# Fused cross-attention and quantised feed-forward on one core: the transposes of an attention slot are moved behind its second scores

## The chip, the core and the metric

The kernel runs on one core of a Trainium2 chip. The metric is the device time of one execution, in microseconds (us). TensorE (PE, with its weight loads as PEld), VectorE (DVE), ScalarE (ACT), GpSimd (POOL) and the DMA queue of SyncE (SP) each work through a list of their own and meet at semaphores.

## The reference

x has the shape (2, 2048, 512), the context (2, 77, 384). All values are float32.

```python
def block(x, ctx):
    q = layernorm(x) @ Wq                 # 16 heads of 32
    k, v = ctx @ Wk, ctx @ Wv             # 77 keys
    attn = softmax(q @ k.T * 32 ** -0.5)
    x = x + tanh(g_xattn) * ((attn @ v) @ Wo)
    xq = fake_quant(layernorm(x))         # one scale over the whole tensor
    h = fake_quant(silu(xq @ wg.T) * (xq @ wu.T))
    return x + tanh(g_ffn) * (h @ wd.T)   # wg, wu, wd quantised by rows
```

## The kernel before

The 4096 rows are 32 tiles of 128. Three stages follow each other: attention, then the gate and up products, then the down product. The second stage needs the maximum over all normalised rows, so no work of it starts before the attention stage has ended.

The attention stage is a software pipeline of 36 slots. Each engine has a function `slot(n, t)`, and `tile_slots` runs it for n from 0 to 35 (slots 8 to 19 in a hardware loop). In slot n TensorE works on several tiles at once:

- `scores(n, 0)` and `scores(n, 1)`: the two halves of the heads of tile n, six products each, into the two banks of `p_s`. VectorE takes the maximum by head from them (`scores_max`, L786) and subtracts it into `prob` (`scores_sub`, L797); ScalarE takes the exponential (L632).
- `queries(n + 2, ...)`: 24 products of 256 columns into `p_q`. ScalarE rounds the result (`q_part`, L628), VectorE takes the rest (L771). In even slots they also wait for `x_part(n + 3)` on VectorE (L764), which is the last instruction of VectorE's list of the slot before.
- `prob_transpose(n - 1, 1)`: five transposes (L1129) of the second half of the probabilities, copied out of PSUM by ScalarE's `prob_copy` (L637). The first half goes another way: GpSimd splits it into planes (`prob_split`), SP transposes it by DMA (`prob_transposed`, L430), and ScalarE joins the planes (`prob_join`, L642).
- `outputs(n - 1, 0)` and `outputs(n - 1, 1)` (L1140): ten instructions each, probabilities by values. VectorE divides by the sum (`outputs_rec`, `outputs_norm`, L805 and L810).
- `out_transpose(n - 2)`: four transposes (L1156) of the attention output, taken by ScalarE (L656) and VectorE (`out_part`, L820).
- `project(n - 2)`: twelve products of 512 columns into `p_y`. VectorE adds the row (L917) and takes its statistics in slot n + 1; `row_abs` on ScalarE (L670) and `row_max` on VectorE (L878) of slot n + 2 take the maximum of the normalised row, by way of `p_y`.

Transposes and outputs have plain float32 operands; scores, queries and projection have operands split into two rounded parts, of type fp32r, and take three products for one.

The order of the work is written out by hand for each engine. Slots 4 to 29 are those in which the first half of the probabilities of tile n - 1 comes by DMA and is not the last of its kind; TensorE's list there is `behind_planes`. Slot 30 has a list of its own in that function: both transposes, both outputs, then the second scores. In slots 0 to 21 VectorE and GpSimd also quantise one 128-row block of the gate and up weights (L939, L953, L961), and in slots 22 to 29 (`down_part`, `down_scale`) the four row blocks of the down weights, whose loads SP issues (`down_rows`, L474) behind its transposes and the stores of the block before.

SP's own list does not change. It holds, for each slot, the transpose of a weight block, `planes_transposed(n + 4)`, `prob_transposed(n)` and the load of the next weight block, and `prob_transposed` waits before it starts:

```python
sp.wait_ge(g_ppl, n - PROB0 + 1)
sp.wait_ge(a_p, 2 * n)
```

`a_p` counts ScalarE's `prob_copy` and `prob_join`, two for each tile.

Of the kernel before, what the change touches and what calls it, by code (L numbers as in the profile page):

```python
# [72 lines left out]
def flamingo_block(nc, x, ctx_in, mask, g_xattn, g_ffn, Wq, Wk, Wv, Wo, clip_x, clip_down,  # L73
# [8 lines left out]
    with top:  # L82
# [30 lines left out]
        with attn:  # L113
# [17 lines left out]
            with work:  # L131
# [222 lines left out]
                def late_tile(m):  # L354
                    return isinstance(m, int) and m >= NT - 2
# [19 lines left out]
                def row(n):  # L375
                    return x1[:, span(n), :].rearrange("p a d -> p (a d)")
# [226 lines left out]
                def _(act):  # L603
# [35 lines left out]
                    def prob_join(m):  # L639
                        wait(act, d_pT, 16 * (m - PROB0) + 16)  # L640
                        wait(act, t_o, 2 * m - 1)
                        act.copy(pT_pairs, ppl_T).then_inc(a_p, 1)  # L642

                    def slot(n, t):
                        if last_by_dma(n):
                            prob_join(n - 1)
                        if isinstance(n, int) and n == 2:
                            prob_copy(n - 1, 0)
                            prob_copy(n - 1, 1)
                        if isinstance(n, int) and n in (NT - 1, NT):  # L650
                            prob_copy(n - 1, 0)
                        if runs(n - 2, NT):
                            wait(act, t_oT, n - 1)
                            if not late_tile(n - 2):
                                wait(act, t_y, n - 2)
                            act.copy(oT(n - 2)[0], p_x[:, :, :]).then_inc(a_ohi, 1)  # L656
                        if isinstance(n, int) and n == 1:
                            act.wait_ge(l_v[0], 16 * SLOT0[KB])
                        if runs(n - 1, NT) and not (isinstance(n, int) and n == 2):
                            if not by_dma(n - 1) and not (isinstance(n, int) and n in (NT - 1, NT)):  # L660
                                prob_copy(n - 1, 0)
                            prob_copy(n - 1, 1)
                        if runs(n - 4, NT - 1):
                            wait(act, g_nb2, n - 3)
                            wait(act, v_xmax, n - 3)
                            if isinstance(n, int) and n >= PLANES_FREE:
                                act.wait_ge(v_xlo, NT)
                            else:
                                wait(act, v_x1, n - 2)
                            act.activation(xabs(n - 4), row(n - 4), ACT.Abs, bias=nb2[:, span(n - 4)],  # L670
                                           scale=rs2[:, span(n - 4)]).then_inc(a_abs, 1)
# [5 lines left out]
                        if runs(n - 1, NT) and by_dma(n - 1) and not last_by_dma(n):  # L677
                            prob_join(n - 1)
# [11 lines left out]
                        if isinstance(n, int) and 1 <= n <= 4:  # L690
                            if n == 1:
                                act.wait_ge(t_v, B)
                                act.wait_ge(v_wq, KD)
                            four = slice(8 + 4 * n, 12 + 4 * n)
                            act.dma_start(x1[:, four, :], x_v[:, four, :]).then_inc(l_x[4], 16)
                        if isinstance(n, int) and n == 5:
                            act.wait_ge(g_wo, 1)
                            act.dma_start(x1[:, NT - KD:NT, :], x_v[:, NT - KD:NT, :]).then_inc(l_x[5], 16)
# [46 lines left out]
                def _(dve):  # L745
# [134 lines left out]
                    def last_slot(n, t):  # L880
# [14 lines left out]
                        dve.wait_ge(a_abs, n - 3)  # L895
                        dve.tensor_reduce(xmax[:, span(n - 4)], xabs(n - 4), X, ALU.max).then_inc(v_xmax, 1)

                    def slot(n, t):
                        if isinstance(n, int) and n == NT + 1:
                            out_part(NT - 1)  # L900
                            row_max(n - 4)
# [169 lines left out]
                def _(pe):  # L1071
# [59 lines left out]
                        last.then_inc(t_p, 1)  # L1131

                    def outputs(n, half):
                        wait(pe, a_p, 2 * n + (2 if by_dma(n) and not last_by_dma(n + 1) else 1 + half))
                        wait(pe, v_o, 2 * n - 1 + half)
                        b = n // (S // P)
                        for j in range(KB):
                            first, end = heads_of(j)
                            rows = slice(0, ROWS[j])
                            last = pe.matmul(  # L1140
                                p_o[half][:, first:end + 1, :].rearrange("p h d -> p (h d)"),
                                pT[rows, half * KB + j, :],
                                vblk[rows, span(b), half, SLOT0[j]:SLOT0[j + 1], :]
                                .rearrange("p a s d -> p (a s d)"),
                                start=(j == 0), stop=(j == KB - 1), skip_group_check=True)
# [641 lines left out]
```

## Time and profile before

| | |
|---|---|
| time, median of 3 runs | 616.19 us (615.35 to 618.91) |
| the profiled execution's own time | 615.18 us |
| its span, first to last instruction | 613.4 us |
| TensorE busy | 599.6 us, 98% of the span |
| VectorE busy | 518.3 us, 84% |
| ScalarE busy | 376.0 us, 61% |
| GpSimd busy | 234.9 us, 38% |
| slots 4 to 29 | 64.24 to 339.60 us of the span |
| second stage | its first product starts at 376.33 us |

Times in the rows are counted from the start of the span. A row of a timeline gives start, duration, engine, line and operation; the time from one start to the next tells more of a pipelined engine than the durations, which overlap. TensorE's clock was granted in full through slots 4 to 29.

### The profile page before, as it was taken

The numbers are of one execution on the slowest core, as the hardware profiler recorded it, in microseconds if no ns is written. First come the engines' busy times: TensorE is split into PE (matmuls) and PEld (weight loads), VectorE is DVE, ScalarE is ACT, GpSimd is POOL, SyncE is SP. The second block draws the span as 40 slices with busy tenths as digits, with TensorE's granted clock in tenths as the row PEclk, the third lists the DMA queues.
The fourth block names the chain that finished last, engine by engine and source line by source line (L and its number), as shares of the span: only waits on it lengthen the run. The fifth ranks groups of instructions, "written<-read, shape, count | busy, mean of one in ns | idle before, by whom it ended". The sixth has DMA issues, their size and how long they took to land. (4 is left out here: it accounts for less than half of the span.)

```text
span 613.4 us, 12115 instructions
## 1 busy us (share of the span) xinstructions
PE 599.6 (98%) x3727; PEld 446.5 (73%) x3727; DVE 518.3 (84%) x957; ACT 376.0 (61%) x484; POOL 234.9 (38%) x473
## 2 busy tenths in 40 slices
PE   8999999999999999999999997999999999899997
PEld 6799999999999999999999873444444444444544
DVE  6788899999999998999999877888888888856765
ACT  5554677777777777877775535555555554455653
POOL 6253454544544454544533112111011110067775
PEclk9999999999999999999999998999999999999999
DMA  8534785354434445534642000496642110199633
GB/s 318 172 117 119 197 193 115 84 106 89 89 89 95 95 84 109 113 70 112 139 92 61 27 1 10 114 229 219 210 173 67 35 34 1 45 368 399 251 120 120
DMA packets 118507, 77.89 MB, mean 127 GB/s; under 512 B 98211, under 2 KB 100669, under 8 KB 118461
## 3 DMA queue, kind: packets, MB, share of 16 engines
q1 hardware_dynamic: 113169, 60.51, 38.6%
q10 hardware_dynamic: 5292, 16.82, 7.4%
q8 instruction: 23, 0.38, 0.2%
q14 instruction: 23, 0.19, 0.1%
HBM read 32.48 MB, written 21.36 MB: 88 GB/s over the span
## 5 line engine op out<-in xcount | busy, mean ns | idle before, releaser
L1459 ACT ACTIVATE sb_silu<-ps_g,sb_sgu 128x512 f32<-128x512 f32 x88 | 60.5, 688 | 72.0 <-PE ps_g L1554 43.4
L1554 PE MATMUL ps_g<-sb_xqT,sb_wgu 128*128 128x512 bf16 x352 | 90.3, 379 | 0.6 <-DVE sb_xqT L1510 0.6
L1554 PE MATMUL ps_u<-sb_xqT,sb_wgu 128*128 128x512 bf16 x352 | 90.3, 379 | 0.0
L1525 DVE SCALAR_TENSOR_TENSOR sb_h<-ps_u,sb_sgu,sb_silu 128x512 f32<-128x512 f32 (+1 forms) x88 | 66.1, 751 | 19.8 <-PE ps_u L1554 19.3
L1074 PE MATMUL ps_q<-sb_xT_hi,sb_wq_hi 128*128 128x256 f32 x256 | 75.4, 294 | 0.7 <-DVE sb_xT_lo L764 0.6
L1635 POOL TENSOR_TENSOR sb_wgu<-sb_wgu,sb_x 128x512 f32<-128x512 f32 x31 | 53.6, 1730 | 52.6 <-DVE sb_wgu L1692 52.6
L632 ACT ACTIVATE sb_prob<-sb_prob 128x616 f32<-128x616 f32 x64 | 45.6, 713 | 44.3 <-DVE sb_prob L797 44.3
L1076 PE MATMUL ps_q<-sb_xT_hi,sb_wq_lo 128*128 128x256 f32 x256 | 72.4, 283 | 0.0
L1075 PE MATMUL ps_q<-sb_xT_lo,sb_wq_hi 128*128 128x256 f32 x256 | 72.3, 283 | 0.0
L1759 PE MATMUL ps_z<-sb_wdT,sb_hq 128*128 128x512 bf16 x330 | 71.9, 379 | 0.2
L1529 DVE TENSOR_REDUCE sb_hmax<-sb_h 128x1 f32<-128x512 f32 (+1 forms) x88 | 60.4, 686 | 7.6
L1554 PEld LDWEIGHTS ps_g<-sb_xqT,sb_wgu 128*128 128x128 bf16 x352 | 34.4, 98 | 42.0 <-ACT sb_xqT L1476 0.8
L1554 PEld LDWEIGHTS ps_u<-sb_xqT,sb_wgu 128*128 128x128 bf16 x352 | 34.4, 98 | 41.5
L786 DVE TENSOR_REDUCE sb_smax<-ps_s 128x8 f32<-128x616 f32 x64 | 50.9, 796 | 15.1 <-PE ps_s L1119 15.0
L1759 PEld LDWEIGHTS ps_z<-sb_wdT,sb_hq 128*128 128x128 bf16 x330 | 31.9, 98 | 39.8 <-ACT sb_hq L1655 2.3
L1442 POOL CAST sb_xqb<-sb_xq 128x512 bf16<-128x512 int8 x28 | 17.2, 614 | 112.3 <-ACT sb_xq L1451 93.7
L1655 ACT CAST sb_hq<-sb_h 128x1408 bf16<-128x1408 int8 (+1 forms) x32 | 42.0, 1312 | 28.0 <-DVE sb_h L1685 27.9
L797 DVE TENSOR_TENSOR sb_prob<-ps_s,sb_smax 128x616 f32<-128x616 f32 x64 | 51.2, 800 | 1.8
L1074 PEld LDWEIGHTS ps_q<-sb_xT_hi,sb_wq_hi 128*128 128x128 f32 x256 | 48.9, 191 | 1.4 <-DVE sb_xT_lo L764 0.8
L1074 PE MATMUL ps_y<-sb_wo_hi,sb_oT_hi 128*128 128x512 f32 x120 | 49.9, 416 | 0.0
L1075 PEld LDWEIGHTS ps_q<-sb_xT_lo,sb_wq_hi 128*128 128x128 f32 x256 | 49.0, 192 | 0.2 <-issue 0.2
L1076 PEld LDWEIGHTS ps_q<-sb_xT_hi,sb_wq_lo 128*128 128x128 f32 x256 | 48.9, 191 | 0.0
(238 smaller groups left out, 1422.7 us busy)
## 6 DMA issues: line engine op xcount, KB each, us to landing
h_spill<-sb_h SPq DMA_DIRECT2D x4, 2816.0 KB, 9.5
sb_h<-h_spill ACTq DMA_DIRECT2D x16, 704.0 KB, 7.1
out_dram<-sb_wgu SPq DMA_DIRECT2D x31, 256.0 KB, 2.2
sb_x<-in_x_dram ACTq DMA_DIRECT2D x5, 1024.0 KB, 6.1
sb_w_in<-in_L_ffn_w_gate_dram SPq DMA_DIRECT2D x11, 256.0 KB, 2.8
sb_w_in<-in_L_ffn_w_up_dram SPq DMA_DIRECT2D x11, 256.0 KB, 2.6
sb_x<-in_x_dram SPq DMA_DIRECT2D x2, 1024.0 KB, 14.0
sb_x<-in_x_dram SPq DMA_DIRECT2D x2, 512.0 KB, 4.4
```

The costliest lines, as they stand in the source:

```text
L632: act.activation(prob[:, half, :], prob[:, half, :], ACT.Exp, scale=SCALE).then_inc(a_exp, 1)
L786: dve.tensor_reduce(smax[:, half, :].rearrange("p (g h) -> p g h", g=2), half_scores(), X, ALU.max).then_inc(v_max, 1)
L797: dve.tensor_tensor(prob[:, half, :].rearrange("p (g h m) -> p g h m", g=2, h=HG), half_scores(), smax[:, half, :].rearrange("p (g h) -> p ...
L1074: pe.matmul(o, hi, rhi, start=first, stop=False)
L1075: pe.matmul(o, hi, rlo, start=False, stop=False)
L1076: return pe.matmul(o, lo, rhi, start=False, stop=last)
L1459: act.activation(silu[(j * KI + i) % 2][:, :, :].rearrange("p t n -> p (t n)"), p_g[(j * KI + i) % 2][:, :], ACT.Silu, scale=sgu[:, i:i + ...
L1525: dve.scalar_tensor_tensor(steps_h, p_u[(j * KI + i) % 2][:, :, :], sgu[:, KI + i:KI + i + 1], silu[(j * KI + i) % 2][:, :, :], ALU.mult, ...
L1529: dve.tensor_reduce(hmax[:, span(u)], steps_h, mybir.AxisListType.XY, ALU.max, apply_absolute_value=True).then_inc(v_hmax, 1)
L1554: last = pe.matmul(banks[(j * KI + i) % 2][:, :], wgu[:, what, k, i * P:(i + 1) * P], xqT[j][:, k, :], start=(k == 0), stop=(k == KD - 1))
L1635: pool.tensor_tensor(yd[k], yd[k], x1[:, span((v + RT) % NT), :].rearrange("p a d -> p (a d)"), ALU.add).then_inc(g_out, 1)
L1759: last = pe.matmul(p_z[k % 4][:, :], hq[k % 4][:, i, :], wdT[:, i, :], start=(i == 0), stop=(i == KI - 1))
```

## The change

In slots 4 to 29 TensorE's list is put in another order. Before: first scores, transposes of the output, transposes of the probabilities, queries, second scores, a quarter of the projection, both outputs, the rest of the projection. After: first scores, queries, second scores, transposes of the output, transposes of the probabilities, both outputs, the whole projection. `outputs` now waits for each half's own count of `a_p`.

ScalarE gets a list for these slots, `planes_slot`: the join of the planes comes first (before, it followed the first exponential), so it counts in `a_p` ahead of `prob_copy`; the copy of the transposed output and `prob_copy` come behind `q_part` instead of at the slot's head.

VectorE gets one too: the addition of the row comes ahead of the first maximum, the rest of the queries ahead of the second maximum, and `out_part` between the second maximum and its subtraction. The instructions and their numbers are the same on every engine. The cut diff:

```diff
 # tensor
 def behind_planes(n, t):
-        out_transpose(n - 2)
-        prob_transpose(n - 1, 1)
         if last_by_dma(n):
+            out_transpose(n - 2)
+            prob_transpose(n - 1, 1)
             outputs(n - 1, 0)
...
                 queries(n + 2, (t + 2) % 4, part)
         scores(n, t, 1)
-        project(n - 2, [0])
+        out_transpose(n - 2)
+        prob_transpose(n - 1, 1)
         outputs(n - 1, 0)
         outputs(n - 1, 1)
-        project(n - 2, range(1, KD))
+        project(n - 2)
 def outputs(n, half):
-        wait(pe, a_p, 2 * n + (2 if by_dma(n) and not last_by_dma(n + 1) else 1 + half))
+        wait(pe, a_p, 2 * n + 1 + half)
 # scalar
+def planes_slot(n, t):
+        prob_join(n - 1)
+        if runs(n - 4, NT - 1):
+            row_abs(n - 4)
+        exponential(n, 0)
+        if runs(n + 2, NT):
+            q_part(n + 2, (t + 2) % 4)
+        out_high(n - 2)
+        prob_copy(n - 1, 1)
+        if runs(n + 4, NT):
+            x_join(n + 4, t)
+        exponential(n, 1)
+        if runs(n + 5, NT):
+            normalise(n + 5, t + 5)
 # vector
+def planes_slot(n, t):
+        m = n - 3
+        wait(dve, t_y, m + 1)
+        dve.tensor_tensor(row(m), y_full(m)[:, 0:D], row(m), ALU.add).then_inc(v_x1, 1)
+        scores_max(n, 0)
+        wait(dve, v_x1, m + 1)
+        wait(dve, v_st2, m)
+        scores_sub(n, t, 0)
+        dve.bn_stats(bn2[:, 0, :], row(m)).then_inc(v_bn2, 1)
+        wait(dve, v_bn2, m + 1)
+        wait(dve, g_nb2, m)
+        if runs(n - 4, NT):
+            row_max(n - 4)
+        dve.bn_aggr(mvt[:, :], bn2[:, 0, :]).then_inc(v_st2, 1)
...
+        down_part(n, 0)
...
+        if runs(n + 2, NT):
+            q_part(n + 2, (t + 2) % 4)
+        scores_max(n, 1)
+        out_part(n - 2)
+        scores_sub(n, t, 1)
...
+        outputs_rec(n - 1, 0)
+        outputs_norm(n - 1, 0)
+        outputs_rec(n - 1, 1)
...
```

## Rows read from the trace of the kernel before

**Rows 1.** Windows, slots 4 to 21 and 22 to 29: length, then busy time by engine.

```profile
64.24:254.59 190.35, 190.35 (x1387) 180.69 (x1386) 175.76 (x360) 142.33 (x180) 91.92 (x232) 1.00 0.51 109
254.59:339.60 85.01, 85.01 (x617) 80.24 (x616) 80.01 (x163) 59.16 (x75) 36.24 (x85) 1.00 0.46 99
```

**Rows 2.** Waits, 60 to 330 us: who waited for whom, total, times, longest.

```profile
DVE sb_smax L786 <- PE ps_s L1119: 11.2, 20, 1.9
```

**Rows 3.** Timeline of TensorE, slot 13: transposes, then queries.

```profile
160.66 0.71 PE L1129 MATMUL ps_p<-sb_identf,sb_prob 128*128 128x128 f32 x5
161.13 0.36 PE L1074 MATMUL ps_q<-sb_xT_hi,sb_wq_hi 128*128 128x256 f32 x1
161.33 0.28 PE L1075 MATMUL ps_q<-sb_xT_lo,sb_wq_hi 128*128 128x256 f32 x1
161.45 0.28 PE L1076 MATMUL ps_q<-sb_xT_hi,sb_wq_lo 128*128 128x256 f32 x1
```

**Rows 4.** Timeline of TensorE, slot 3: transposes before outputs, scores before queries.

```profile
55.99 0.71 PE L1129 MATMUL ps_p<-sb_identf,sb_prob 128*128 128x128 f32 x5
56.53 1.23 PE L1140 MATMUL ps_o<-sb_vblk,sb_pT 128*128 128x66 f32 x10
...
58.36 0.30 PE L1119 MATMUL ps_s<-sb_k_hi,sb_q_lo 128*128 128x308 f32 x1
58.50 0.28 PE L1074 MATMUL ps_q<-sb_xT_hi,sb_wq_hi 128*128 128x256 f32 x1
```

**Rows 5.** Timeline of TensorE, slot 12: outputs, then the projection's rest.

```profile
156.12 1.28 PE L1140 MATMUL ps_p<-sb_vblk,sb_pT 128*128 128x66 f32 x10
157.20 0.48 PE L1074 MATMUL ps_y<-sb_wo_hi,sb_oT_hi 128*128 128x512 f32 x1
157.52 0.39 PE L1075 MATMUL ps_y<-sb_wo_lo,sb_oT_hi 128*128 128x512 f32 x1
157.75 0.40 PE L1076 MATMUL ps_y<-sb_wo_hi,sb_oT_lo 128*128 128x512 f32 x1
```

**Rows 6.** Timeline of slot 30, TensorE, its weight loads and ScalarE.

```profile
341.43 1.23 PE L1140 MATMUL ps_o<-sb_vblk,sb_pT 128*128 128x66 f32 x10
342.50 1.28 PE L1140 MATMUL ps_p<-sb_vblk,sb_pT 128*128 128x66 f32 x10
342.44 1.20 PEld L1140 LDWEIGHTS ps_p<-sb_vblk,sb_pT 128*128 128x128 f32 x10
341.63 0.69 ACT L637 COPY sb_pT<-ps_p 128x640 f32<-128x640 f32 x1
```

**Rows 7.** Waits of the SP queue, 60 to 340 us.

```profile
SPq L429 <- ACT sb_pT L642: 66.1, 26, 8.2
```

**Rows 8.** The tile sb_ppl, 100 to 300 us: DMA from issue to landing.

```profile
DMA to landing us min/median/max: 3.3/3.3/4.1
```

**Rows 9.** Timeline of VectorE, turn of slots 12 and 13.

```profile
159.42 0.66 DVE L764 TENSOR_TENSOR sb_xT_lo<-sb_xpl,sb_xT_hi 128x512 fp32r<-128x512 f32 x1
160.43 0.80 DVE L786 TENSOR_REDUCE sb_smax<-ps_s 128x8 f32<-128x616 f32 x1 [0.35 <-PE ps_s L1119]
161.14 0.68 DVE L917 TENSOR_TENSOR sb_x<-ps_y,sb_x 128x512 f32 x1
```

**Rows 10.** Timeline of VectorE, slot 22: its maxima and a subtraction; slots 23, 24.

```profile
255.64 0.80 DVE L786 TENSOR_REDUCE sb_smax<-ps_s 128x8 f32<-128x616 f32 x1 [0.68 <-PE ps_s L1119]
...
260.36 0.80 DVE L786 TENSOR_REDUCE sb_smax<-ps_s 128x8 f32<-128x616 f32 x1
261.19 0.80 DVE L797 TENSOR_TENSOR sb_prob<-ps_s,sb_smax 128x616 f32<-128x616 f32 x1
...
266.57 0.79 DVE L786 TENSOR_REDUCE sb_smax<-ps_s 128x8 f32<-128x616 f32 x1
...
276.88 0.80 DVE L786 TENSOR_REDUCE sb_smax<-ps_s 128x8 f32<-128x616 f32 x1
...
302.86 0.69 DVE L827 TENSOR_REDUCE sb_wd_am<-sb_w_in 128x1 f32<-128x512 f32 x1 [0.71 <-DMA sb_w_in<-in_L_ffn_w_down_dram]
```

More of the change, by code:

```diff
@@ L642, in prob_join, with x_load @@
                         act.copy(pT_pairs, ppl_T).then_inc(a_p, 1)
-                    def slot(n, t):
+                    def x_load(n):
+                        if isinstance(n, int) and 1 <= n <= 4:
+                            if n == 1:
+                                act.wait_ge(t_v, B)
+                                act.wait_ge(v_wq, KD)
+                            four = slice(8 + 4 * n, 12 + 4 * n)
+                            act.dma_start(x1[:, four, :], x_v[:, four, :]).then_inc(l_x[4], 16)
+                        if isinstance(n, int) and n == 5:
+                            act.wait_ge(g_wo, 1)
+                            act.dma_start(x1[:, NT - KD:NT, :], x_v[:, NT - KD:NT, :]).then_inc(l_x[5], 16)
@@ new lines, in row_abs @@
+                    def row_abs(m):
+                        wait(act, g_nb2, m + 1)
+                        wait(act, v_xmax, m + 1)
+                        if isinstance(m, int) and m + 4 >= PLANES_FREE:
+                            act.wait_ge(v_xlo, NT)
+                        else:
+                            wait(act, v_x1, m + 2)
+                        act.activation(xabs(m), row(m), ACT.Abs, bias=nb2[:, span(m)],
+                                       scale=rs2[:, span(m)]).then_inc(a_abs, 1)
@@ new lines, in out_high @@
+                    def out_high(m):
+                        wait(act, t_oT, m + 1)
+                        if not late_tile(m):
+                            wait(act, t_y, m)
+                        act.copy(oT(m)[0], p_x[:, :, :]).then_inc(a_ohi, 1)
+                    def planes_slot(n, t):
[12 more added lines that the diff above has]
+                            normalise(n + 5, t + 5)
@@ L645, in slot @@
+                    def slot(n, t):
+                        if by_dma(n - 1) and not last_by_dma(n):
+                            planes_slot(n, t)
+                            if isinstance(n, int) and n in (4, 5):
+                                x_load(n)
+                            return
                         if last_by_dma(n):
@@ L652, in slot @@
                         if runs(n - 2, NT):
[L653 to L656, printed above, removed]
+                            out_high(n - 2)
                         if isinstance(n, int) and n == 1:
@@ L663, in slot @@
                         if runs(n - 4, NT - 1):
[L664 to L671, printed above, removed]
+                            row_abs(n - 4)
                         if runs(n, NT):
@@ L676, in slot @@
                             act.copy(wo_hi[:, :, :], wo_raw).then_inc(a_wo, 1)
-                        if runs(n - 1, NT) and by_dma(n - 1) and not last_by_dma(n):
-                            prob_join(n - 1)
                         if runs(n + 2, NT):
@@ L689, in slot @@
                             normalise(n + 5, t + 5)
[L690 to L698, printed above, removed]
+                        if isinstance(n, int) and 1 <= n <= 3:
+                            x_load(n)
                     act.dma_start(mask_u, mask.rearrange("(a b) m -> a (b m)", a=1)).then_inc(l_mask, 16)
@@ L896, in last_slot @@
                         dve.tensor_reduce(xmax[:, span(n - 4)], xabs(n - 4), X, ALU.max).then_inc(v_xmax, 1)
+                    def planes_slot(n, t):
[12 more added lines that the diff above has]
+                        dve.bn_aggr(mvt[:, :], bn2[:, 0, :]).then_inc(v_st2, 1)
+                        if runs(n, NW):
+                            wait(dve, d_w, 16 * n + 16)
+                            wait(dve, g_sc, n)
+                            dve.tensor_reduce(w_am[:, :], w_in[:, :], X, ALU.max, apply_absolute_value=True)\
+                               .then_inc(v_wam, 1)
+                        down_part(n, 0)
+                        if runs(n, NW):
+                            wait(dve, v_wam, n + 1)
+                            wait(dve, v_wi8, n)
+                            dve.reciprocal(w_inv[:, :], w_am[:, :]).then_inc(v_winv, 1)
+                        if runs(n + 2, NT):
[3 more added lines that the diff above has]
+                        scores_sub(n, t, 1)
+                        if runs(n, NW):
+                            wait(dve, v_winv, n + 1)
+                            wait(dve, g_wbf, n)
+                            dve.tensor_scalar(w_i8[:, :], w_in[:, :], w_inv[:, :], QMAX, ALU.mult, ALU.mult)\
+                               .then_inc(v_wi8, 1)
+                        down_part(n, 1)
+                        down_part(n, 2)
+                        down_scale(n)
+                        if runs(n + 6, NT):
+                            wait(dve, v_st, n + 6)
+                            if isinstance(n, int) and n + 6 == 12:
+                                dve.wait_ge(l_x[4], 16 * 4)
+                            if isinstance(n, int) and n + 6 == NT - KD:
+                                dve.wait_ge(l_x[5], 16)
+                        outputs_rec(n - 1, 0)
+                        outputs_norm(n - 1, 0)
+                        outputs_rec(n - 1, 1)
+                        if runs(n + 6, NT):
+                            stats(n + 6)
+                            wait(dve, v_bn, n + 7)
+                            wait(dve, g_nb, n + 5)
+                        outputs_norm(n - 1, 1)
+                        if runs(n + 6, NT):
+                            stats_end(n + 6, t)
+                        if runs(n + 4, NT):
+                            x_part(n + 4, t)
@@ L898, in slot @@
                     def slot(n, t):
+                        if by_dma(n - 1) and not last_by_dma(n):
+                            planes_slot(n, t)
+                            return
                         if isinstance(n, int) and n == NT + 1:
```

## The prediction

> **What bounds the kernel now.** I read the windows first: in slots 4 to 21 TensorE is busy for the whole 190.35 us, VectorE for 175.76, ScalarE for 142.33; the clock is full [rows 1]. Divided by 18 that is 10.575 us a slot, of which VectorE fills 9.76 by the same row. In slots 22 to 29 TensorE is again busy throughout, but the slot is 85.01 / 8 = 10.626 us: 8 x 0.051 = 0.41 us of stretched products hide there, and VectorE is at 80.01 of 85.01. Then the waits: VectorE waits for the scores of TensorE, 11.2 us in 20 waits, and no wait of TensorE of any size stands against it [rows 2]. So TensorE's issue sets the slot, VectorE is 0.4 to 0.6 us behind it, and the change can win only if TensorE's own list gets shorter, or lose if a new order makes TensorE wait. The timelines then say what one switch costs and how late each partner may be. Nothing after slot 29 changes; the second stage waits for all rows, so a microsecond of a slot is a microsecond of the end.
>
> **TensorE's list.** The same instructions are issued; only the neighbours change. The removed neighbourhood is transposes to queries. It looks dear: the first query takes 0.36 us against 0.28, and the next one starts 0.20 us later instead of 0.12 (161.13, 161.33, 161.45) [rows 3]. But the five transposes before it take only 161.13 - 160.66 = 0.47 us from start to start, while in front of outputs the same five take 56.53 - 55.99 = 0.54 [rows 4]. Both together: 0.47 + 0.20 = 0.67 with the switch, 0.54 + 0.12 = 0.66 without. The cost is 0.01 us; most of what one row shows is given back by the row ahead. The dearer switch is outputs to projection: 1.08 + 0.32 us against 1.07 + 0.23, some 0.10 us [rows 5, 6], and the new order keeps one of it a slot. Scores to queries, which is new here, costs 0.14 us, the ordinary spacing of scores [rows 4]. The whole slot, from starts: scores 12 x 0.141 = 1.69, queries 24 x 0.12 = 2.88, nine transposes 9 x 0.108 = 0.97, outputs 1.07 + 1.08 = 2.15, projection 0.32 + 11 x 0.2325 = 2.88 (0.23 is 157.75 - 157.52). Sum 10.57 us, against 10.575 now. I take -0.015 us x 26 = -0.4 us. Bounds: -0.08 x 26 = -2.1 us if the first query's 0.08 is all real, +0.02 x 26 = +0.5 us for the rounding of the rows.
>
> **The new short path: transposes, copy, outputs.** Call the start of the first scores 0. Then queries start at 0.85, second scores at 3.73, output transposes at 4.58, probability transposes at 5.01, outputs at 5.55 and 6.62, projection at 7.70. Before, some 4.5 us lay between the probability transposes and the outputs that use them; now the second outputs follow 1.6 us behind, and `prob_copy` lies between, queued on ScalarE behind `q_part` and the copy of the output. Slot 30 of the old kernel has just this order. There the copy starts at 341.63 and ends at 342.32, the weight load that needs it is at 342.44, and the outputs start at 342.50, 1.07 us behind the first ones (341.43), which is their own length [rows 6]. So the wait is nothing, with 0.12 us from the copy's end to the load. That holds if ScalarE is free when the transposes end: `q_part` starts at about 3.95 (queries end) and ends at 4.55; the copy of the output can start at 5.21. I take 0. Bounds 0 and, if the copy came 0.1 us later in each slot, 26 x 0.1 = +2.6 us.
>
> **SP and the join.** `prob_transposed(n)` waits until `a_p` is 2n. Today the last to count is the join (66.1 us of waits in 26 slots) [rows 7], 5.7 us into the slot. With the join first, the last to count is `prob_copy`, which ends at 6.45: the transposing DMA starts 0.7 us later. It lands 3.3 us behind its issue, 4.1 at worst [rows 8], so at 9.8 to 10.6. The join wants it when ScalarE is through its list, at about 9.7, some 0.1 us late, at worst 0.9. Behind the join stand `row_abs` (`row_max` wants it at 3.3 of the next slot, it ends at 1.7) and the first exponential, which waits for VectorE until 2.7 anyway. The loop join, `row_abs`, exponential, `q_part`, two copies, DMA is about 4.6 + 3.4 = 8.0 us round, under 10.57. Queued on SP behind this DMA are the next weight load and weight transpose; their own waits end later (8.0 and 8.8), so they keep their times. Cost 0.
>
> **VectorE, slots 4 to 21.** The addition now starts at 0.20, when the projection ends, where the first maximum had to wait until 160.43, 1.05 into its slot [rows 9]. The list gets waits on itself: maximum then subtraction with nothing between costs 261.19 - 260.36 = 0.83 us instead of about 0.71 (161.14 - 160.43) [rows 9, 10]; `row_max` straight behind the statistics, and the reciprocal straight behind its maximum, I estimate at the same 0.11 each. So +0.2 to +0.3 us a slot on a list that ended 0.35 us before the slot did: it comes to about 10.35 of 10.57, idle included. TensorE's deadlines against it: even queries want `x_part` by 0.72 of the slot, and it ends near 0.05 (before: 160.08, that is 0.70, wanted at 1.70); second scores want the subtraction by 3.6, it ends at 2.7; the projection wants `out_part` by 7.56, it ends at 6.9. Cost 0; bound above: 0.1 us a slot, 18 x 0.1 = +1.8 us.
>
> **VectorE, slots 22 to 29.** Here it has no slack: from first maximum to first maximum slot 22 takes 10.93 us and slot 23 10.31, without a wait [rows 10]. The pair is 21.24 against TensorE's 21.15. The new waits add about 0.15 (two of 0.11 to 0.12 come, one goes since `out_part` parts the second pair): 11.08 and 10.46. How late VectorE begins a slot, L: 0 at slot 22, then 0.14 idle + 11.08 - 10.57 = 0.65 at 23, 0.54 at 24. Even queries are the tight deadline, since they moved 0.9 us forward: `x_part` ends at 0.27 + L, plus 0.05 to be seen, wanted by 0.72, so L above 0.40 is paid. Slot 24 pays 0.14, L is 0.91 at 25, slot 25 some 0.1 for `out_part`, slot 26 0.35. Then the loads of the down weights: in slot 26 the first reduction waits 0.71 us for DMA until 302.86, 5.8 into the slot [rows 10]; it is now due at 4.3, and the rest of the queries, the second maximum and `out_part` (0.60 + 0.60 + 0.72 + 0.73 us) stand behind it, so the projection goes at 8.45 instead of 7.56: 0.9 us. Loads of the other three blocks landing near their old time I price at 0.3 together. Sum 0.14 + 0.1 + 0.35 + 0.9 + 0.3 = 1.8, less the 0.41 that is lost now [rows 1]: +1.4 us. Bounds: -0.4 if no lag is left, +3.0 if each of three loads costs what slot 26's does.
>
> The Trainium skill ("VectorE: DVE Perf Modes", The DRAIN you can't avoid) says that chained VectorE instructions cost the same with a semaphore after each as without. By that rule the 0.15 a slot would be gone and L would stay near 0.5 at slot 24 and 0.7 at slot 26, the lag near 0.3 us instead of 0.6, and the sum 0.3 lower. The pair at 0.83 against 0.71 speaks against it.
>
> **Sum.** -0.4 + 0 + 0 + 0 + 1.4 = +1.0 us. The profiled execution took 615.18 us (span 613.4), so 616.2 for it; it lies 1.0 us under the median of 616.19, so I forecast **617.2 us** for the median, +0.16%. A measurement of this kernel tells about 0.5%, 3.1 us, from no change.
>
> **Rivals.**
> (1) The switch is real: TensorE gains the 0.08 us of the first query in 26 slots, -2.1 us, and the lag of slots 22 to 29 vanishes because `out_transpose` no longer waits for VectorE's division, -0.4: 613.7 us, faster by 0.4%. For it: the 0.36 us row. Against: the 0.47 ahead of it [rows 3, 4].
> (2) The second outputs wait for `prob_copy`. The margin is 0.12 us [rows 6]; it decides as soon as ScalarE begins the copy of the output over 0.1 us late. With 0.2 us a slot: +5.2 + 1.0 = 622.4 us, slower by 1.0%. Against: ScalarE has 0.65 us idle ahead of that copy.
> (3) VectorE becomes the bound in slots 4 to 21 too: its list is 0.2 us under the slot; if three more self-waits or a late weight load add 0.35, the slot is 10.7: 18 x 0.15 + 1.0 = 619.9 us.
> (4) The loads of slots 22 to 29 land early enough: the 0.9 + 0.3 go, 616.0 us. For it: slot 26's is the only such wait of the old trace [rows 10].
>
> **Chances.** Forecast 0.42; (4) 0.16; (1) 0.14; (2) 0.13; (3) 0.15. The range must reach (1) and (3) and the lower part of (2): 613.6 to 621.0; the likeliest case alone has 616.0 to 618.9. Faster by over 0.5% (below 613.1) needs (1) and more: 0.09. Slower by over 0.5% (above 619.3) is (2), over half of (3) and the top of the forecast's bound: 0.25. The rest, 0.66, is no change.
>
> **What would show it.** Right: in slots 5 to 21 output transposes start 10.56 to 10.58 us apart; five transposes before outputs 0.54 us, queries 0.12 throughout; second outputs 1.07 us behind the first; SP's L429 waits for L637 instead of L642; small stretches of TensorE before even queries and before the projection in slots 24 to 27, and VectorE's L827 waiting for DMA longer than 0.71 us. Wrong: a slot of 10.50 or less, or of 10.7 or more, before slot 22; a wait of L1140's weight load for ScalarE L637.

## The result and the profile after

The kernel after the change takes **618.22 us** (median of 20 runs, 616.76 to 622.82); the kernel before, on the same chip, 615.73 us (20 runs, 615.02 to 620.21). The ratio is 1.0037, with an interval of 1.0023 to 1.0051: 2.5 us slower. That is too little to tell from no change by the bound of 0.5%, and 1.0 us above the forecast of 617.2. The profiled execution took 617.91 us, span 616.0, so 2.73 us more than the profiled execution of before.

The page's first part, busy time by engine:

```profile
PE 601.0 (98%) x3727; PEld 447.6 (73%) x3727; DVE 519.5 (84%) x957; ACT 382.2 (62%) x484; POOL 234.8 (38%) x473
```

The shares hardly moved. ScalarE has 6 us more, 4 of them in slots 4 to 29; where they come from isn't shown, its join has kept its mean length of 1.66 us. The difference is found by stage. The windows of after, slots 4 to 21, slots 22 to 29, and then slot 28 by itself:

```profile
64.51:255.08 190.57, 190.57 (x1387) 180.74 (x1386) 176.91 (x360) 146.38 (x181) 91.17 (x232) 1.00 0.50 109
255.08:342.80 87.72, 86.23 (x618) 80.70 (x617) 80.11 (x163) 59.16 (x74) 36.41 (x85) 1.00 0.43 96
...
320.09:332.19 12.10, 10.80 (x78) 10.12 (x77) 9.20 (x20) 7.05 (x9) 3.42 (x8) 1.00 0.42 117
```

Against [rows 1] the first eighteen slots take 190.57 us for 190.35, 0.2 us more, and TensorE is busy for all of it. The last eight take 87.72 for 85.01: 2.7 us, the whole difference. What follows slot 29 is the same, 26.62 us from slot 30 to the last product of the stage for 26.63. Slot by slot, from the first product of the first scores to that of the next slot, in us:

| slot | 22 | 23 | 24 | 25 | 26 | 27 | 28 | 29 | sum |
|---|---|---|---|---|---|---|---|---|---|
| before | 10.59 | 10.65 | 10.59 | 10.65 | 10.59 | 10.78 | 10.58 | 10.58 | 85.01 |
| after | 10.58 | 10.91 | 10.95 | 11.03 | 10.94 | 10.60 | 12.10 | 10.61 | 87.72 |

There are two losses: slots 23 to 26 are each 0.3 to 0.45 us over a free slot of 10.58 (1.5 us together), and slot 28 is 1.5 us over.

TensorE in slot 13 of after, to be laid beside [rows 3 to 5]; start, duration, line and operation, with groups of equal rows cut:

```profile
160.46 0.30 PE L1206 MATMUL ps_s<-sb_k_hi,sb_q_lo 128*128 x1
160.60 0.28 PE L1161 MATMUL ps_q<-sb_xT_hi,sb_wq_hi 128*128 128x256 f32 x1
160.72 0.28 PE L1162 MATMUL ps_q<-sb_xT_lo,sb_wq_hi 128*128 128x256 f32 x1
...
164.31 0.60 PE L1243 MATMUL ps_x<-sb_identf,sb_o_sb 128*128 128x128 f32 x4
164.75 0.71 PE L1216 MATMUL ps_p<-sb_identf,sb_prob 128*128 128x128 f32 x5
165.29 1.23 PE L1227 MATMUL ps_o<-sb_vblk,sb_pT 128*128 x10
166.36 1.29 PE L1227 MATMUL ps_p<-sb_vblk,sb_pT 128*128 x10
167.46 0.47 PE L1161 MATMUL ps_y<-sb_wo_hi,sb_oT_hi 128*128 128x512 f32 x1
167.77 0.39 PE L1162 MATMUL ps_y<-sb_wo_lo,sb_oT_hi 128*128 128x512 f32 x1
```

The first query is now 0.28 us long and the next one starts 0.12 us later, but the five transposes take 165.29 - 164.75 = 0.54 us where they took 0.47. The second outputs start 1.07 us behind the first and the projection 1.10 behind them: no wait for `prob_copy`.

The waits of after between 60 and 345 us (who for whom: total, times, longest):

```profile
ACT sb_pT L642 <- DMA sb_ppl<-sb_ppl: 9.6, 23, 2.2
DVE sb_prob L825 <- DVE sb_smax L814: 5.2, 26, 0.2
DVE sb_wd_am L855 <- DMA sb_w_in<-in_L_ffn_w_down_dram: 3.0, 4, 2.3
DVE sb_smax L814 <- PE ps_s L1206: 2.6, 7, 1.6
PEld ps_y L1161 <- DVE sb_oT_lo L848: 1.6, 2, 1.4
PE ps_y L1161 <- DVE sb_oT_lo L848: 1.3, 1, 1.3
PEld ps_q L1161 <- DVE sb_xT_lo L792: 0.7, 2, 0.3
```

VectorE's waiting for the scores has shrunk: over 60 to 330 us it was 11.2 [rows 2] and is 0.9; the 2.6 shown here have 1.6 from slot 30. In its place stand 26 waits of 0.2 us on its own maximum, and 3.0 us on loads of the down weights: 0.20 in slot 22, 0.24 in slot 24, 0.26 in slot 26 and 2.30 in slot 28. ScalarE's join now waits for its DMA in 23 slots, 9.6 us in all, where the kernel before had one such wait of 0.9; TensorE has no wait on ScalarE among its own. It now waits for VectorE, at the projection (1.3) and at the even queries (0.7, seen on its weight loads). The bound is still TensorE, but in slots 23 to 26 and in slot 28 VectorE now holds it up.

VectorE of after at the start of slot 13, in slots 23 and 24 and in slot 28 (in brackets the idle time ahead of an instruction, and what ended it):

```profile
160.18 0.68 DVE L929 TENSOR_TENSOR sb_x<-ps_y,sb_x 128x512 f32 x1
160.80 0.80 DVE L814 TENSOR_REDUCE sb_smax<-ps_s 128x8 f32<-128x616 f32 x1
161.80 0.80 DVE L825 TENSOR_TENSOR sb_prob<-ps_s,sb_smax 128x616 f32<-128x616 f32 x1 [0.20 <-DVE sb_smax L814]
...
270.59 1.11 DVE L863 TENSOR_SCALAR sb_w_i<-sb_w_in,sb_wd_inv 128x512 int8<-128x512 f32 x1
...
281.16 0.17 DVE L939 BATCH_NORM_AGGREGATE sb_mvt<-sb_bn 128x2 f32<-128x6 f32 x1
281.57 0.69 DVE L855 TENSOR_REDUCE sb_wd_am<-sb_w_in 128x1 f32<-128x512 f32 x1 [0.24 <-DMA sb_w_in<-in_L_ffn_w_down_dram]
...
326.65 0.69 DVE L855 TENSOR_REDUCE sb_wd_am<-sb_w_in 128x1 f32<-128x512 f32 x1 [2.30 <-DMA sb_w_in<-in_L_ffn_w_down_dram]
327.26 0.68 DVE L799 TENSOR_TENSOR sb_q_lo<-ps_q,sb_q_hi 128x512 fp32r<-128x512 f32 x1
327.85 0.79 DVE L814 TENSOR_REDUCE sb_smax<-ps_s 128x8 f32<-128x616 f32 x1
328.56 0.68 DVE L848 TENSOR_TENSOR sb_oT_lo<-ps_x,sb_oT_hi 128x512 fp32r<-128x512 f32 x1
```

Four things are to be seen. From maximum to subtraction it is now 161.80 - 160.80 = 1.00 us, where the prediction took 0.83; the maximum, though, starts 0.62 us behind the addition, where the addition started 0.71 behind the maximum before. The scaling to int8 of slot 23 takes 1.11 us, where the same place of the list took 0.74 before. In slot 24 the reduction of a down block starts 281.57 - 281.16 = 0.41 us behind the instruction ahead of it, because it waits for its load. And in slot 28 the reduction of a down block waits 2.30 us for its load, with the rest of the queries, the second maximum and `out_part` queued behind; `out_part` ends at 329.24, 9.15 us into the slot, and TensorE's projection has stood still for it:

```profile
326.71 1.28 PE L1227 MATMUL ps_p<-sb_vblk,sb_pT 128*128 128x66 f32 x10
329.30 0.50 PE L1161 MATMUL ps_y<-sb_wo_hi,sb_oT_hi 128*128 128x512 f32 x1 [1.30 <-DVE sb_oT_lo L848]
```

Why that load is late is read on SP's queue and on GpSimd. SP of after ahead of slot 28 (the second column is the issue's length), then its counterpart of before, then GpSimd of after:

```profile
316.01 1.35 SPq L430 DMA_TRANSPOSE sb_ppl<-sb_ppl  x1
317.40 4.60 SPq L480 DMA_DIRECT2D wd_spill<-sb_w_bf  x2
322.05 0.43 SPq L474 DMA_DIRECT2D sb_w_in<-in_L_ffn_w_down_dram  x1
```

```profile
313.72 1.35 SPq L430 DMA_TRANSPOSE sb_ppl<-sb_ppl  x1
315.74 3.32 SPq L480 DMA_DIRECT2D wd_spill<-sb_w_bf  x2
319.11 0.43 SPq L474 DMA_DIRECT2D sb_w_in<-in_L_ffn_w_down_dram  x1
```

```profile
321.03 0.62 POOL L577 CAST sb_w_bf<-sb_vblk 128x512 bf16<-128x512 int8 x1 [4.33 <-DMA wd_spill<-sb_w_bf]
```

SP issues the transpose of the probabilities later in the slot (6.5 to 6.9 us into it, before 5.7 to 6.1), because it waits for `prob_copy` instead of the join: 94.0 us in 26 slots where it was 66.1 [rows 7]. Behind it stand the two stores of the quantised block. The second store needs GpSimd's second cast, the cast needs the first store landed (4.33 us of waiting, where it was 2.38 before), and the next load stands behind the second store. The load is issued 1.96 us into slot 28, before 0.67. So 1.3 of the 2.30 us are the later issue; the rest is that VectorE, with its new list, is at the reduction 4.3 us into the slot, before 5.0.

### The profile page after: what moved, and what is told of

It reads as the page before. It is cut to its first block and busy times, and to the rows that moved or that the text cites. A ratio compares the mean times of both kernels' runs of the same rounds, so it can differ in the third digit from the quotient of the medians.

```text
span 616.0 us, 12121 instructions
## 1 busy us (share of the span) xinstructions
PE 601.0 (98%) x3727; PEld 447.6 (73%) x3727; DVE 519.5 (84%) x957; ACT 382.2 (62%) x484; POOL 234.8 (38%) x473
## 5 line engine op out<-in xcount | busy, mean ns | idle before, releaser
L1612 DVE SCALAR_TENSOR_TENSOR sb_h<-ps_u,sb_sgu,sb_silu 128x512 f32<-128x512 f32 (+1 forms) x88 | 66.1, 751 | 19.7 <-PE ps_u L1641 18.8
L1161 PE MATMUL ps_q<-sb_xT_hi,sb_wq_hi 128*128 128x256 f32 x256 | 73.3, 286 | 1.0 <-DVE sb_xT_lo L792 0.6
L642 ACT COPY sb_pT<-sb_ppl 128x1280 uint16<-128x1280 uint16 x27 | 44.9, 1662 | 9.6 <-DMA sb_ppl<-sb_ppl 9.6
```

What stands on the lines that cost most here:

```text
L1161: pe.matmul(o, hi, rhi, start=first, stop=False)
L1612: dve.scalar_tensor_tensor(steps_h, p_u[(j * KI + i) % 2][:, :, :], sgu[:, KI + i:KI + i + 1], silu[(j * KI + i) % 2][:, :, :], ALU.mult, ...
```

## The experiments

In each table the slots are those of the profiled execution. Its load times scatter: one or two of the slots 26 to 28 may be 1 to 2 us longer or shorter in another execution, so the row of slots tells where time is lost and the ratio tells how much. Slots 4 to 21 took 190.4 to 190.6 us in all that keep the new lists, and are not repeated.

**old_tail.** The new order in slots 4 to 21 only; slots 22 to 29 have the old lists on all engines.

```diff
-if by_dma(n - 1) and not last_by_dma(n):
+if by_dma(n - 1) and not last_by_dma(n) and n < 22:      # on every engine
```

> Slots 4 to 21 as changed, slots 22 to 29 with the old lists on all three engines. Theory A (the whole loss is made in slots 22 to 29, where VectorE is full and the down weights are loaded): the 2.7 us lost there come back, slots 4 to 21 keep their 10.58 us, and the kernel is within 0.1% of the one before the change, 615.5 to 616.3. Rival B (the new order itself costs, spread over all 26 slots, or after them): slots 4 to 21 hold two thirds of it, and the kernel stays some 1.5 us over the one before.

Measured: 616.29 us against 615.72, ratio 1.0014 (0.9992 to 1.0037); windows, slots 22 to 29:

```profile
255.06:340.44 85.38, 85.02 (x618) 80.26 (x617) 79.61 (x163) 59.00 (x74) 36.25 (x85) 1.00 0.45 99
```

Slots 4 to 21 keep 190.57 us, and the eight last ones are back at 85.38; the 0.37 us over the kernel before are all in slot 27 (11.16 for 10.78), behind a wait for a load of 1.10 us in slot 26. Where VectorE has slack the new order costs no more than 0.2 us in eighteen slots and gains nothing; the loss lies in slots 22 to 29.

**sp_join.** SP's transpose waits for the join only, as it did before.

```diff
-sp.wait_ge(a_p, 2 * n)
+sp.wait_ge(a_p, 2 * n - (n > PROB0))
```

> The changed kernel, but SP's transpose of the probabilities waits for the join alone (2n - 1), not for the copy behind it. Theory A: the DMA starts about 5.0 us into a slot instead of 6.5, the stores and loads of the down weights queued behind it go 1 to 3 us earlier, the 2.3 us wait of VectorE in slot 28 goes and with it the 1.5 us of that slot; the lag of slots 23 to 26 (some 1.5 us) stays: 1.2 to 1.6 us faster than the changed kernel, about 1.0 us over the one before. Rival C (the late load of slot 28 is contention of transfers, not the queue): the wait moves or stays, no gain.

**max_first.** In slots 23 to 26 the first maximum goes ahead of the addition, so that VectorE has an instruction between maximum and subtraction.

```diff
+if 23 <= n <= 26: scores_max(n, 0)
 dve.tensor_tensor(row(m), y_full(m)[:, 0:D], row(m), ALU.add)
-scores_max(n, 0)
+if not 23 <= n <= 26: scores_max(n, 0)
```

> The changed kernel, but in slots 23 to 26 VectorE takes the first maximum ahead of the addition, so that the addition stands between the maximum and its subtraction. Theory A: each of the four slots gets 0.2 to 0.28 us of VectorE back, TensorE's stretch in them falls from 1.5 us to about 0.5, slot 28 keeps its 1.5: 0.8 to 1.1 us faster than the changed kernel. Rival D (these slots are late for the queries' wait on x_part or another engine, whatever VectorE's length): no change in slots 23 to 26.

**both.** The two edits together.

> Both edits, the wait for the join alone and the first maximum ahead in slots 23 to 26. Theory A: they add up, 2.2 to 2.6 us faster than the changed kernel, within 0.1% of the one before. If TensorE's order were worth anything by itself, this kernel would be faster than the one before; by the rows it is worth 0.0 +/- 0.5 us.

| | median (before) | ratio | slots 22 to 29 |
|---|---|---|---|
| sp_join | 616.98 | 1.0027 (1.0009 to 1.0044) | 10.58, 10.89, 10.96, 10.66, 10.93, 10.60, 10.65, 10.59 = 85.86 |
| max_first | 618.62 | 1.0053 (1.0032 to 1.0073) | 10.58, 10.59, 10.94, 11.21, 10.96, 10.60, 11.37, 10.60 = 86.85 |
| both | 616.74 | 1.0013 (0.9995 to 1.0032) | 10.58, 10.71, 10.93, 10.58, 10.94, 10.58, 10.81, 10.58 = 85.71 |

The windows of sp_join, slots 22 to 29:

```profile
255.53:341.39 85.86, 85.70 (x618) 80.59 (x617) 79.98 (x163) 59.35 (x74) 36.67 (x85) 1.00 0.42 99
```

With SP's earlier wait, slot 28 falls from 12.10 to 10.65 and the wait for its load from 2.30 to 0.84 us. One execution of each could be scatter, so all kernels are laid side by side. With SP's early wait (here, in `both` and in the next two) the load is issued 0.86 to 1.31 us into slot 28, VectorE waits 0.84 to 1.56 us for it and the slot takes 10.65 to 11.36. With the late wait (after, `max_first`, `more_switches`) it is 1.43 to 1.96, 1.56 to 2.30 and 11.37 to 12.10. The second loss is SP's wait for the larger part.

Slots 23, 24 and 26 keep their loss, but slot 25 falls from 11.03 to 10.66. That is a load too. In slot 24 the reduction now finds its block landed, and VectorE's list of that slot is shorter by 0.37 us (10.96 for 11.33, from addition to addition):

```profile
281.60 0.17 DVE L939 BATCH_NORM_AGGREGATE sb_mvt<-sb_bn 128x2 f32<-128x6 f32 x1
281.69 0.65 DVE L855 TENSOR_REDUCE sb_wd_am<-sb_w_in 128x1 f32<-128x512 f32 x1
```

`max_first` missed what was expected of it: it frees slot 23 (10.91 to 10.59) and no more, and its median isn't below that of the changed kernel. The edit itself is worth some 0.18 us in slot 23, as `both` shows against `sp_join` (10.71 for 10.89); the rest of the 0.32 lies in a wait for the load of slot 22 that this execution didn't have. In slot 24 VectorE, being earlier, waits 0.68 us for the load instead of 0.24, and slot 25 takes 11.21. Slots 24 and 26 stay at 10.93 to 10.96 in both kernels that have the edit: there the queries wait for `x_part`, at the end of VectorE's list. `both` was expected 2.2 to 2.6 us faster than the changed kernel; it is so by 1.5 us in the medians and 2.0 in the slots.

**join_xpart.** As sp_join, and `x_part(n + 4)`, which the even queries of the next slot wait for, goes ahead of `outputs_rec` from slot 22 on.

```diff
+if n >= 22: x_part(n + 4, t)
 outputs_rec(n - 1, 0)
...
-x_part(n + 4, t)
+if n < 22: x_part(n + 4, t)
```

> The kernel in which SP waits for the join alone, and in slots 22 to 29 VectorE takes the rest of the transposed row (x_part) ahead of the four reciprocals and divisions instead of at the end of its list, some 1.9 us earlier. Theory A (even slots pay because their queries, moved 0.9 us forward, wait for x_part): slots 24 and 26 fall from 10.95 to about 10.6; the lag itself stays, so slots 23 and 25 still pay for out_part or the second scores, 10.7 to 10.9. Slots 22 to 29 take 85.2 to 85.5 us instead of 85.86. Rival E (even slots pay for something else that is behind VectorE): slots 24 and 26 stay at 10.9.

Measured: 617.10 us against 615.79, ratio 1.0020 (1.0000 to 1.0041); slots 10.58, 10.91, **10.59**, 11.03, 10.87, 10.80, 11.04, 10.60 = 86.42. Slot 24 is free at once, so its 0.37 us had been the deadline of the even queries, as the prediction had it. Slots 23 and 25 keep their loss; 0.21 us of it in each lies ahead of the projection, which wants `out_part`, the rest at the second scores. The sum was expected at 85.2 to 85.5 and missed it, because VectorE waits 0.25, 0.55 and 1.23 us for loads in slots 22, 26 and 28. It isn't earlier at the reduction of slot 26 than in `sp_join` (4.77 us into the slot, 4.67 there); the block is there later, 5.4 us behind its issue.

**all_three.** SP's wait, the maximum first, and the early `x_part`.

> The wait for the join alone, the first maximum ahead in slots 23 to 26, and x_part ahead of the divisions in slots 22 to 29. Theory A: no deadline of TensorE is missed by more than 0.1 us, slots 22 to 29 take 84.7 to 85.1 us, the same as before the change (85.01); the time equals the one before within 0.1%. Rival B (the new order of TensorE costs by itself): over 85.5.

Measured: 618.04 us against 615.79, ratio 1.0034 (1.0021 to 1.0047); slots 10.58, 10.64, 10.59, 10.79, **11.96**, 10.81, 11.36, 10.60 = 87.33. The expectation was missed. The first four slots are nearly free, but the gain is given back: VectorE's reduction waits for loads, 3.4 us in three waits, the longest 1.7 us in slot 26. There SP's issue of the load takes 2.07 us; in all other blocks of this run it is 0.43 to 0.52. What held it isn't shown.

```profile
DVE sb_wd_am L855 <- DMA sb_w_in<-in_L_ffn_w_down_dram: 3.4, 3, 1.7
```

```profile
298.23 2.07 SPq L474 DMA_DIRECT2D sb_w_in<-in_L_ffn_w_down_dram  x1
```

**late_down.** The changed kernel, with the first block work of slots 22, 24, 26 and 28 behind the second subtraction, so that nothing TensorE wants soon is queued behind the wait for the load.

```diff
-down_part(n, 0)
+if wd_step(n)[1] != 0: down_part(n, 0)
 ...
 scores_sub(n, t, 1)
+if wd_step(n)[1] == 0: down_part(n, 0)
```

> The changed kernel, but in slots 22, 24, 26 and 28 VectorE's first reduction of the down weights (down_part 0) moves from ahead of the queries' rest to behind the second subtraction, beside the other two. Theory A: in these slots nothing that TensorE waits for stands behind the load any more; the waits of VectorE for it (3.0 us in four slots, 2.3 of them in slot 28) shrink under 0.3, slot 28 falls from 12.1 to about 10.6 us; slots 23 to 26 keep most of their lag. Slots 22 to 29 take 86.0 to 86.4 us instead of 87.7, and the kernel is 1.2 to 1.6 us faster than the changed one. Rival F (the load's landing is only the sign of a late store chain that holds something else up): slot 28 stays over 11.

Measured: 617.05 us against 616.09, ratio 1.0027 (1.0006 to 1.0047); slots 10.58, 10.96, 10.97, 10.89, 10.96, 10.60, **10.60**, 10.60 = 86.16. VectorE's wait for loads is gone, though SP still waits for `prob_copy`. Slots 23 to 26 lose as much as in the changed kernel; in slots 22 and 28 a wait of 0.27 and 0.28 us for ScalarE's part of the queries stands where the wait for the load was. So the second loss goes without the first, as in slots 22 to 25 of `all_three` the first went without the second.

**all_four.** All of these together.

> All four edits: SP waits for the join alone, first maximum ahead in slots 23 to 26, x_part ahead of the divisions and down_part 0 behind the second subtraction in slots 22 to 29. Theory A: slots 22 to 29 take 84.7 to 84.9 us, which is TensorE's own list, against 85.01 before the change; the kernel's time equals the one before within 0.1%, so that the order of TensorE is worth nothing and everything the change lost was waits. Rival B: over 85.5 us, or a slower kernel all the same.

Measured: 616.01 us against 616.09, ratio 1.0005 (0.9979 to 1.0031); slots 10.58, 10.74, 10.60, 10.77, 10.60, 10.58, 10.58, 10.58. Windows, slots 4 to 21 and 22 to 29:

```profile
64.69:255.27 190.58, 190.58 (x1388) 180.74 (x1386) 176.76 (x360) 144.87 (x181) 91.53 (x232) 1.00 0.50 109
255.27:340.30 85.03, 85.03 (x617) 80.40 (x616) 80.22 (x163) 59.00 (x74) 37.20 (x85) 1.00 0.43 100
```

TensorE is busy for all of both stretches, and they are as long as before the change within 0.2 us [rows 1]. The last eight slots stay 0.13 us above the 84.9 that were expected at most; slots 23 and 25 still lose 0.16 and 0.19. With the two losses away or nearly so the new order of TensorE is worth 0: it equals the kernel before and doesn't beat it.

**more_switches.** One run. The changed kernel, with the output transposes between the two halves of the queries: each slot has one more pair of changes between plain float32 and fp32r.

```diff
 for part in range(2):
     queries(n + 2, (t + 2) % 4, part)
+    if part == 0: out_transpose(n - 2)
 scores(n, t, 1)
-out_transpose(n - 2)
```

> The changed kernel, but the four transposes of the output stand between the two halves of the queries in slots 4 to 29, which puts one more switch from float32 to fp32r products into each slot. By the prediction a switch behind transposes costs 0.01 us: slots 4 to 21 at 10.58 to 10.60. Rival 1 of the prediction (0.08 us of the first product behind it are real): 10.66 or more, 1.5 us over slots 4 to 21. The query behind the transposes should last 0.36 us and have its neighbour 0.20 us behind it in either case.

Measured: 617.46 us, one run; slots 4 to 21 190.41 us. TensorE's rows around the added change, slot 14:

```profile
172.33 0.60 PE L1243 MATMUL ps_x<-sb_identf,sb_o_sb 128*128 128x128 f32 x4
172.69 0.36 PE L1161 MATMUL ps_q<-sb_xT_hi,sb_wq_hi 128*128 128x256 f32 x1
172.89 0.28 PE L1162 MATMUL ps_q<-sb_xT_lo,sb_wq_hi 128*128 128x256 f32 x1
```

Four transposes take 172.69 - 172.33 = 0.36 us and the query behind them 0.20: 0.56 us, and four at 0.108 with one query at 0.12 are 0.55. One more change in each of eighteen slots makes them 0.16 us shorter together, if anything. The 0.36 us row is no price: the transposes ahead of it have given back what it shows.

**block_alone.** One run. The kernel before with one edit: the quarter of the projection that stood between second scores and outputs goes to the rest of it.

```diff
 scores(n, t, 1)
-project(n - 2, [0])
 outputs(n - 1, 0)
 outputs(n - 1, 1)
-project(n - 2, range(1, KD))
+project(n - 2)
```

> The kernel before the change with one edit: the projection's first quarter moves behind the outputs, so that it is one block; transposes and lists of ScalarE and VectorE stay. By the prediction it changes nothing in slots 4 to 29 (275.4 us before): one product's spacing stays 0.23 us wherever it stands, the switch behind the outputs stays. Rival: leaving the switch between projection and outputs out saves 0.05 us or more a slot, 274 us or less.

Measured: 625.50 us, one run, slots of 10.78 to 11.19 us. The expectation was missed. The join's row and the rows of TensorE around the outputs, and then the waits:

```profile
167.69 1.65 ACT L642 COPY sb_pT<-sb_ppl 128x1280 uint16<-128x1280 uint16 x1
169.07 0.30 PE L1119 MATMUL ps_s<-sb_k_hi,sb_q_lo 128*128 x1
169.60 1.32 PE L1140 MATMUL ps_o<-sb_vblk,sb_pT 128*128 x10 [0.23 <-ACT sb_pT L642]
```

```profile
PEld ps_o L1140 <- ACT sb_pT L642: 2.9, 14, 0.4
PE ps_o L1140 <- ACT sb_pT L642: 2.5, 12, 0.4
```

The quarter had covered the end of the join, which ends at 169.34, where the outputs would have started at 169.21. With the join behind the first exponential the block of the projection costs 0.2 to 0.6 us a slot; the changed kernel, with the join at the head of ScalarE's list, has it for nothing.

**old_scalar_list.** One run. The changed kernel with ScalarE's old list, and the outputs waiting for both halves as before.

> The changed kernel with ScalarE's list as before the change (the copy of the output and prob_copy at its head, the join behind the first exponential), and outputs waiting for both as before. ScalarE then sits at its head until the output transposes end at 5.2 us, the copies, row_abs, exponential and join end at about 9.3, and the outputs, due at 5.55, start there: by theory A each of the 26 slots grows by some 3.8 us, 100 us in all. If ScalarE's list were of no weight, 10.6 us.

Measured: 805.02 us, one run, slots of 17.4 to 18.9 us; the expectation had 3.8 us a slot more, and 7.2 came. Waits, then windows of two stretches (behind the POOL column stand the granted clock and the DMA's share):

```profile
ACT sb_oT_hi L669 <- PE ps_x L1240: 182.2, 25, 8.3
PE ps_o L1224 <- ACT sb_pT L642: 88.7, 24, 3.8
```

```profile
100.00:200.00 100.00, 77.66 (x436) 71.62 (x435) 54.26 (x109) 43.44 (x56) 28.53 (x73) 0.81 0.32 63
200.00:300.00 100.00, 81.12 (x433) 74.69 (x433) 56.49 (x114) 42.24 (x54) 28.80 (x74) 0.77 0.28 59
```

ScalarE stands at the head of its list for transposes that TensorE now makes behind the second scores; the join, `q_part` and the copies stand behind, and TensorE waits for them in turn: a closed loop. Its gaps are 3.7 us a slot (88.7 in 24), and the rest of the 7.2 comes with a granted clock that fell to 0.77 to 0.81 of full speed. ScalarE's new list is no ornament of the change: without it the new order of TensorE costs 187 us.

## Why the prediction was right, and by how much its terms were off

The forecast was 617.2 us in a range of 613.6 to 621.0, with no measurable change the likeliest; 618.22 came, also inside the likeliest case's own 616.0 to 618.9. The change itself was forecast at +1.0 us and came at +2.5 by the medians and +2.7 in the profiled executions. That the time is only 1.0 us off owes something to luck: the forecast stood on a median of three runs of the kernel before, 616.19, and that of twenty is 615.73. By its steps:

- **TensorE's list**: -0.4 us forecast with bounds of -2.1 and +0.5, +0.2 measured over slots 4 to 21. A slot took 10.58 us where the sum gave 10.57. The reading that the long first query is given back by shorter transposes held to 0.01 us, in after and in `more_switches`, so rival 1 is out. The switch from outputs to projection, read as 0.10 us, is still there (1.10 + 0.31 us in slot 13).
- **Transposes, copy, outputs**: 0 forecast, and 0 came. Outputs never waited for `prob_copy` in slots 4 to 29; rival 2 is out. This 0 rests on ScalarE's order: `block_alone` and `old_scalar_list` show what lies on its other side, some 10 and 187 us.
- **VectorE, slots 4 to 21**: 0 forecast, 0 came, though its waits on itself were dearer than assumed. Rival 3 is out for these slots.
- **VectorE, slots 22 to 29**: the mis-sized term. +1.4 us forecast net, +2.7 measured. The mechanism was the one named, even queries and projection late by VectorE, and waits for the down loads. The lag of slots 23 to 26 was priced 0.6 us and cost 1.5. The new waits of VectorE on itself were sized about right: dearer at the first maximum (1.00), cheaper at the addition (0.62 or less) and at the second pair, they add some 0.2 us to a pair of slots where 0.3 was forecast. In `sp_join`, where no load is waited for in slot 24, the pair of slots 24 and 25 takes VectorE 10.96 + 10.64 = 21.60 us, forecast 21.54, before 21.24. In after it takes 11.33 + 10.65 = 21.98. What was too small is the price of the loads, 0.3 us for three blocks: the waits of slots 22 and 24 alone lengthen VectorE's list by some 0.3 and 0.4 us, ahead of slots that have no slack for it, which is the larger part of what is missing. The scalings to int8 weren't in the forecast; 1.11 and 0.47 us for 0.74 and 0.70 add 0.14 to 0.15 a pair.
- **SP and the join**: priced 0, and this is what failed in it: "Queued on SP behind this DMA are the next weight load and weight transpose; their own waits end later (8.0 and 8.8), so they keep their times." In slots up to 21 they moved by 0.4 us (the load is issued 8.26 us into slot 13, before 7.89) and nothing paid for it. The join's wait for its DMA, expected 0.1 us late and at worst 0.9, is up to 2.2, and nothing paid for that either. From slot 22 on it is the stores and loads of the down blocks that are queued there. They moved, slot 28's load by 1.3 us. That slot cost 1.5 us in the profiled execution, where 0.9 had been priced for slot 26, on the ground that VectorE comes earlier; so rival 4 is out as well. `sp_join` shows the cause: 0.84 us of waiting in slot 28 for 2.30, and 1.9 us less in the eight slots, 1.45 of it in slot 28 and 0.37 in slot 25. Its median is 1.2 us below the changed kernel's, with intervals that overlap, so the ratio doesn't settle that size alone.

That both losses are the whole of it is shown from two sides: the old lists in the last eight slots alone (85.38 us), and the new lists with four small edits (85.03), against 87.72 in after and 85.01 before.

The Trainium skill ("VectorE: DVE Perf Modes", The DRAIN you can't avoid) says of eight VectorE copies in a row that a semaphore after each costs nothing extra. For a dependent pair the trace disagrees here: 0.71 us from a maximum to a next instruction that doesn't use it [rows 9], 0.83 to a subtraction that does [rows 10], and 1.00 in after, where the subtraction has two more waits, on the addition and on the statistics. The waits alone don't cost it: with the addition between, as before the change and in `max_first`, the same subtraction with the same waits starts 0.71 us behind the addition. Which of them holds it up right behind the maximum wasn't tried.

What stays open: why the wait of GpSimd's cast for the store grew from 2.38 to 4.33 us, more than the later transpose alone explains (it is 3.5 in `sp_join`, whose transpose is early), what makes a load land or its issue end late in slot 26 of `join_xpart` and `all_three`, and how often slots 26 to 28 lose 1 us or more to loads. `max_first` alone has a median 0.4 us above the changed kernel, where its slots say 0.9 below; the intervals allow both.

## What to carry to other kernels

One row next to a switch of operand types can show a price that the row ahead gives back: take start-to-start times over both neighbours of a switch before counting on its removal. When an order changes on one engine, follow the wait that moves, then everything queued behind it in every stage, not only in the one that was drawn; here the same SP wait was harmless in 18 slots and cost up to 1.5 us in one of the next eight. Where an engine has no slack, taking one lag away shows the next wait; two losses in a row have to go together before the end moves.

## What the runs showed of the hardware

- From the start of a maximum on VectorE to the next instruction: 0.71 us where that one doesn't use it, 0.83 where it is the subtraction that does, 1.00 where the subtraction has two further waits.
- The scaling of a 128x512 block to int8 on VectorE took the longer, the longer GpSimd copied or cast beside it: 1.11 us with 0.84 us of overlap (slot 23 of after, GpSimd's copy of the planes from 270.22 to 271.43), 0.74 with 0.45 and 0.70 with 0.42 (slot 23 of before), 0.47 with none. That the two contend is argued from these overlaps; no run moved one of them alone.
- TensorE's granted clock, 1.00 through slots 4 to 29 in all other kernels, fell to 0.77 to 0.81 between its two levels of 1.2 and 2.4 GHz when each slot had gaps of some 4 us (`old_scalar_list`): a wait of 3.7 us a slot cost 7.2.
- A change from plain float32 transposes to fp32r queries on TensorE costs 0.01 us or nothing, whatever the single row next to it seems to say. One from the outputs of 66 columns to the fp32r projection costs some 0.10 us: 1.10 + 0.31 us from start to start in slot 13 of after, against 1.07 + 0.23.
